# One of two value loads of a tile moves from ScalarE's DMA queue to SyncE's, ahead of the band loads

## The reference

```python
s = attention(xn)                    # 16 heads of 16, 12 samples a query
g = silu(mixture_of_experts(xn))     # top 2 of 8 experts, hidden size 512
x = x + s * g
```

## Time and profile before

| | us |
|---|---|
| median of three runs | 1453.27 |
| the profiled execution's own time | 1458.15 |
| span of its trace | 1456.5 |
| TensorE busy in the span | 1363.9 |
| VectorE busy | 1223.2 |
| ScalarE busy | 802.1 |
| GpSimd busy | 856.9 |

### The profile page before, as it was taken

The page is one execution under the profiler, slowest core; times in us unless marked ns, Lnnn a source line. Parts: engine busy times, 40 slices in busy tenths (PEclk is TensorE's granted clock), DMA queues, the critical chain, the costliest instruction groups (busy, mean ns, idle before and its releaser), DMA issues. The chain is left out here.

```text
span 1456.5 us, 36103 instructions
## 1 busy us (share of the span) xinstructions
PE 1363.9 (94%) x13687; PEld 1092.2 (75%) x13688; DVE 1223.2 (84%) x1697; ACT 802.1 (55%) x1873; POOL 856.9 (59%) x566
## 2 busy tenths in 40 slices
PE   5998999996699999999999999999999989989988
PEld 4864566566588888878888888888888867777766
DVE  7846665644999899998998998999999899999951
ACT  2547677765454545545454545455544537666655
POOL 1000377775477888887877878887787843201121
PEclk9998899997899999999999999999999999999999
DMA  7942456776656786767686676768577759889998
GB/s 232 343 156 89 114 177 190 247 232 201 211 149 192 183 236 164 207 170 240 167 242 176 186 220 146 211 150 247 143 214 215 205 136 261 245 243 234 274 252 161
DMA packets 204251, 293.54 MB, mean 202 GB/s; under 512 B 25601, under 2 KB 161029, under 8 KB 203891
## 3 DMA queue, kind: packets, MB, share of 16 engines
q0 software_dynamic: 65792, 146.59, 39.2%
q1 hardware_dynamic: 110723, 133.04, 28.8%
q10 hardware_dynamic: 27632, 12.64, 3.4%
HBM read 182.83 MB, written 117.74 MB: 206 GB/s over the span
## 5 line engine op out<-in xcount | busy, mean ns | idle before, releaser
L1221 POOL DMA_INDIRECT moe_rows<-expert_mem,token_of x142 | 361.6, 2547 | 94.4 <-issue 46.5
L1498 PE MATMUL pA<-xsT,expert_mem 128*128 128x256 f32 x1136 | 261.9, 385 | 13.7 <-DMA expert_mem<-in_w_l 7.6
L1504 PE MATMUL pY<-expert_mem 128*128 x1136 | 264.2, 386 | 0.0
L1202 POOL DMA_INDIRECT expert_mem<-xn_rows,token_of x138 | 232.4, 1684 | 49.0 <-issue 45.6
L1498 PE MATMUL pB<-xsT,expert_mem 128*128 128x256 f32 x1136 | 256.8, 380 | 0.0
L1498 PEld LDWEIGHTS pA<-xsT,expert_mem 128*128 128x128 f32 x1136 | 218.9, 193 | 45.7 <-issue 10.8
L1504 PEld LDWEIGHTS pY<-expert_mem 128*128 128x128 f32 x1136 | 210.4, 190 | 41.3 <-issue 16.1
L1498 PEld LDWEIGHTS pB<-xsT,expert_mem 128*128 128x128 f32 x1136 | 216.3, 190 | 28.9
L1713 DVE SCALAR_TENSOR_TENSOR parts<-pos_pair,prob 128x768 f32<-128x768 f32 x224 | 197.5, 952 | 0.6
L1341 ACT ACTIVATE expert_mem<-pA,b1sel 128x256 f32<-128x256 f32 x284 | 111.0, 473 | 128.8 <-issue 124.9
L1350 ACT ACTIVATE expert_mem<-pB,b1sel 128x256 f32<-128x256 f32 x284 | 111.2, 475 | 111.0 <-PE pB L1498 111.0
(11 more groups left out here) (212 smaller groups left out, 2234.2 us busy)
## 6 DMA issues: line engine op xcount, KB each, us to landing
expert_mem<-in_w_l POOLq DMA_DIRECT2D x71, 1024.0 KB, 7.3
band<-band_rows SPq DMA_DIRECT2D x256, 96.0 KB, 4.4
S_rows<-expert_mem SPq DMA_DIRECT2D x64, 376.0 KB
band_rows<-wgt SPq DMA_DIRECT2D x12, 1536.0 KB, 7.2
pos_pair<-pos_rows SPq DMA_DIRECT2D x28, 384.0 KB, 5.6
xn_rows<-expert_mem SPq DMA_DIRECT2D x16, 512.0 KB, 5.6
v_rows<-expert_mem SPq DMA_DIRECT2D x16, 512.0 KB, 4.3
moe_rows<-zeros POOLq DMA_DIRECT2D x4, 2048.0 KB
```

The lines of the kernel that those rows point to most:

```text
L1202: nc.gpsimd.indirect_dma_start(out=xs[:, u, s], out_offset=None, in_=dram["xn"], in_offset=bass.IndirectOffsetOnAxis(ap=keep["inv"][:, 2 * ...
L1221: nc.gpsimd.indirect_dma_start(out=dram["moe"], out_offset=bass.IndirectOffsetOnAxis(ap=keep["inv"][:, 2 * n + s:2 * n + s + 1], axis=0), ...
L1498: mm = nc.tensor.matmul(dst[:, c], w1[:, 1 - u, k, o * HID + c * P:o * HID + (c + 1) * P], xsT[:, k], start=(k == 0), stop=(k == KC - 1))
L1504: mm = nc.tensor.matmul(pY[:, s], hid[:, h, c, s * P:(s + 1) * P], w2[:, c, ds(e * D, D)], start=False, stop=(s == 1 and c == HC - 1))
```

## The change

For tiles 4 to 63 SyncE issues the value load e = 0 as soon as the slot is free, ahead of the wait for the stored weights and of the four band loads. ScalarE issues only e = 1. For tiles 0 to 3 nothing changes. The waits, the bytes and the destinations are the same.

```diff
                 else:
                     sp.wait_ge(pv_done, n - BAND_SLOTS + 1)
-                if n < BAND_SLOTS:
-                    for e in range(2):
-                        sp.dma_start(slot_v(f)[e:ROWS:2, :, e * HALF:(e + 1) * HALF], keys_of(n, e)).then_inc(v_loaded[f], 16)
+                for e in range(2 if n < BAND_SLOTS else 1):
+                    sp.dma_start(slot_v(f)[e:ROWS:2, :, e * HALF:(e + 1) * HALF], keys_of(n, e)).then_inc(v_loaded[f], 16)
                 if n // GROUP < BY_SP:
                     sp.wait_ge(w_stored, 16 * (n // GROUP + 1))
...
                 act.wait_ge(pv_done, n - BAND_SLOTS + 1)
-                for e in range(2):
-                    act.dma_start(slot_v(f)[e:ROWS:2, :, e * HALF:(e + 1) * HALF], keys_of(n, e)).then_inc(v_loaded[f], 16)
+                act.dma_start(slot_v(f)[1:ROWS:2, :, HALF:], keys_of(n, 1)).then_inc(v_loaded[f], 16)
```

## The result

The changed kernel takes 1471.14 us (median of 9 runs, 1462.74 to 1483.8) against 1455.79 us of the kernel before in the same comparison (9 runs, 1451.84 to 1459.54). The ratio is 1.0098, 95% interval 1.0075 to 1.0121: the change makes the kernel slower by about 14 us. The forecast was slower, by 9.9 us, and its range of 1453 to 1476 us holds the first result.

What follows compares the result with a forecast made beforehand. TensorE was taken to lose time waiting for band loads, 14.4 us. Issue +6.3, queue place +4.8 and ScalarE -1.2 gave +9.9 us: 1458.15 becomes 1468.0 us, the median 1463.2 us; range 1457 to 1473, reaching to 1453 and 1476.

Steps and rivals of the forecast that it cites:

- The bound: Last stage: TensorE is busy but loses time at single places, ten waits for band loads, 14.4 us in all.
- The issue: SyncE's added value-load issue makes the last band issue 0.63 us later at each of ten TensorE waits: +6.3 us.
- The packets: 208 value packets ahead of the band on SyncE's queue cost 0.6 us in each of eight GpSimd bursts: +4.8 us.
- the quiet row: Trace row with only q1 and q10 at work, by which 208 packets on 16 engines take 0.4 us.
- The sum: Issue, queue place and ScalarE terms together: 6.3 + 4.8 - 1.2 = +9.9 us; chance 0.45.
- ScalarE, forecast -1.2 us: ScalarE issues one value load less, so its copies come earlier and TensorE's 1.2 us of waits for them go.
- Only the issue: Rival: on SyncE only issue time counts, not the place on the queue; +5.1 us, 1458.4 us; chance 0.26.
- Hidden: Rival: GpSimd's last byte sets a burst's landing, so neither issue nor place shows; 1452 us, no change; chance 0.11.
- faster: Rival: ScalarE's queue, with half the packets, empties early in bursts and the band lands sooner; -4.4 us, 1448.9 us; chance 0.08.
- SyncE's queue becomes the bound: Rival: in each of eight bursts every tile waits for 400 packets on SyncE's queue; +31 us, 1484 us; chance 0.10.
- Three equal counts: Sign in the profile after: GpSimd's, SyncE's and ScalarE's queues still move equal numbers of packets in a burst.
- the third rival: The rival also called "faster": the band gets its turns sooner in bursts; -4.4 us, chance 0.08.

Runs made afterwards that it cites:

- e5: The kernel before, unchanged, run again for a trace: 1.0007 of the kernel before.
- e6: The changed kernel, unchanged, run again on another chip: 1.0133 of the kernel before.
- e10: The changed kernel with both value loads issued by SyncE ahead of the band loads, none by ScalarE: 1.0203 of the kernel before.
- e12: The kernel before with one band load of 128 partitions in place of four of 32: 0.9949 of the kernel before, 1447.87 us against 1453.85.
- e1: The kernel before plus a DMA of 16 rows of 64 bytes on SyncE's queue ahead of the band loads of tiles 4 to 63: 1.0051, 8.2 us.
- e9: The kernel of e1 run again on another chip: 1.0043 of the kernel before, 6.3 us.
- e8: The changed kernel with GpSimd's last-stage expert-result loads and accumulating stores cut from 256 to 16 columns: 0.9941 of the kernel before, median 1443.57 us.
- e2: The kernel before plus a 64 KB DMA of 128 rows of 512 bytes on SyncE's queue ahead of the band loads: 1.0092, 14.8 us.
- e3: The changed kernel with SyncE's value load e = 0 behind the four band loads instead of ahead: 1.0041 of the kernel before, 6.6 us.
- e4: The changed kernel without the value load e = 0 of tiles 4 to 63: 0.9975 of the kernel before, -4.0 us.
- e11: The kernel before with SyncE issuing three band loads then value load e = 0, ScalarE the fourth band load then e = 1: 0.9993.

## Why the prediction was right, and where its sizes were off

*The bound.* The waits for the band were what mattered; they took 10.1 us more, beside 12.9 us of longer span. The rest is not all in the waits: the products (line 1532, now 1530) run from 1198.6 to 1446.5 us before and from 1194.6 to 1457.6 after, 247.9 against 263.0 us, 15.1 us more, while the stages ahead of it came 4.0 us sooner in this execution. That e5 begins at 1193.0 us with the kernel unchanged shows that the 4.0 us are not the change's. Of the 15.1 us, 3.0 are busy time of TensorE: the same 4903 matmul records take 234.7 us at a granted clock of 0.93, against 231.7 us at 0.95. The forecast has no term for this. One pair of traces would not show it, since e5, unchanged, has 229.3 us at 0.96 and e6 231.0 at 0.95; but e10, with 39.0 us of waits, has 239.6 us at 0.89, and e12, whose waits for the band are almost gone, 226.9 at 0.98. A wait costs more than its own length where the granted clock is lower behind it, as with the transposes at 1418.32 us, 1.94 us against 1.04.

*The issue, forecast +6.3 us.* The kind was right and the size of one issue too small. The prediction took it that the value load would inherit the short first issue and that the last band issue would come 0.63 us later. It comes 1.0 us later: the value load takes its full 0.61 us, and the first band issue behind it 0.85 instead of 0.59. By the prediction's own sum, ten waits, that is about 10 us; there are 16 waits after the change. e1 and e9 don't confirm the 6.3 us: their 8.2 and 6.3 us stand for an issue of 0.31 us, by the same sum some 3.5 us. e1's interval, 4.5 to 12 us, excludes that, e9's, 3 to 10 us, doesn't. So by e1 the issue and its 32 packets cost more than the issue's length times ten. With the bursts small (e8) it is nearly free; that it costs nothing in the quiet stretch was forecast.

*The packets, forecast +4.8 us within 0 to 31.* That they count at all is shown by e2 beside e1, +6.2 us for 112 packets more at the same issue time, if one lets the packets and not the 63 KB stand for it. Their share in the change is not shown: the estimate from the issue time alone, 13 to 15 us, lies at the lower result of the change (14) and below the higher (19). The prediction takes the 0.6 us a burst from the quiet row, and says that what is lost in turns comes back in part when the burst is over. No run shows that return. The prediction also has nothing for a load behind the tile's own band, and e3 shows that one costs as well, by its issue or its packets.

*The sum.* Issue and packets together were forecast at 11.1 us, with ScalarE 9.9. Measured were 14 and 19 us, the first within the range, the second at 1470.99 us by its median, from 1450.51. The range held because it was wide on the side on which the sum was too small; the split of the sum into 6.3 and 4.8 is not borne out by the runs.

*ScalarE, forecast -1.2 us.* Not seen: its waits were 2.3 us after and 1.9 in e6, against 1.6 before and 2.1 in e5. e4 gives 4.0 us for this side together with 96 KB less a tile, and what ScalarE's shorter queue alone brings was not separated from the bytes.

*The rivals.* "Only the issue" falls in its size, 5.1 us, by the result. In its kind it does not fall for the change: e2 beside e1 shows that more than the issue time can count, but there the bytes grew, and the change's issue time was larger than the rival had it. So the rule of the Trainium skill, "DMA: Bandwidth & Descriptors", section "Issuing engines are not separate DMA queues", that issuing from several engines only saves the sequencer's time, is neither shown nor excluded here. "Hidden" and "faster" fall by the result. The other section's rule of turns, "Queues, rings and completion order", agrees with the counts of the stretches shown for both traces, and not with every stretch of a burst, as said above. "SyncE's queue becomes the bound", 31 us, did not happen with one load; locally it does, the 11.3 us without a pause near 1407 us, and e10 with six issues a tile costs 29.5 us.

*What the after was to show.* Waits near 25 us in more than ten places: 24.5 in 16. Quiet stretch 3.53 us a tile: 3.54. SyncE's own waits down by up to 31 us: down by 37.8, since the change adds 0.89 us of issue a tile and not 0.63, 53 us over 60 tiles, most of it out of these waits. Three equal counts: only two, and not in every stretch; ScalarE's queue moves far fewer. That should have helped the band if the third rival were strong; it did not outweigh what was put in.

Open: how much of the 14 to 19 us is SyncE's added issue time, how much lost turns, and how much issues that stretch in a burst (1.58 us for a value load there). A run that leaves the issues as in the change and takes only the packets away was not made. Open too is why e11 loses on ScalarE what it gains at the band: one of its two waits for the copies is 4.2 us long, and its cause was not looked for.

## What to carry to other kernels

A place on a DMA queue that is free in a quiet stretch need not be free while another queue fills the DMA engines. Read for each load how long it has from the freed buffer to its use (8.33 us here) against its landing in a burst, not in quiet. Put no further load on the queue whose landing is waited for: in this kernel it cost ahead of the band (14 and 19 us) and behind it (6.6 us). Take the cost of an issue from its place in the sequence, since the neighbour's issue can change with it, and check that a small stand-in has the issue time of what it stands for. If a load is late, first try to make it fewer DMAs: one band load in place of four gave back 7.4 us, while none of the runs that put a value load on SyncE's queue gained anything.

## What was not expected of the hardware

On the chip of e1 to e4 the kernel before takes 1607.3 us (30 runs, 1599.38 to 1613.6), on the others 1450 to 1456. The last stage is not longer there: from the first product to the last it is 258.3 us in e1 and 257.5 in e9, the same kernel. The time is lost in the first 500 us: between 0 and 300 us TensorE is busy 206.81 us at a granted clock of 0.84 in e1, against 267.65 us at 0.97 in e9, and the 4096 matmuls of line 685 run from 112.4 to 513.6 us against 109.9 to 359.5.

The longest waits in e1 there have no releaser in the profile ("issue") and belong to the weight loads of line 685, 176.4 us in 143 places up to 560 us of the span. The cause was not sought.

One DMA of 128 partitions of 3072 bytes is issued in 0.54 us (median of 64 in e12), four of 32 partitions with the same bytes in 2.52 us. Nor does the issue follow the bytes otherwise: e2's 64 KB take 0.31 us, as e1's 1 KB do, and the value load's 96 KB 0.61. And it depends on what was issued before it: the first band issue takes 0.47 us at the freed slot and 0.85 behind the change's value load. Why is not known.
